# Graph attention in 128 rounds: the probability blocks of four graphs turned by one instruction a round, with their stores and the first and last rounds rearranged

## The reference, cut to what matters

```python
q, k, v = (split_heads(x @ W.T) for W in (Wq, Wk, Wv))
a = einsum('bhnd,bhmd->bhnm', q, k) * 512 ** -0.5 + 2 * adj     # spatial and edge encoding are both adj
a = where(any(a != 0, axis=-1), a, -inf)                        # rows that are all zero give p = 0
p = softmax(a)
o = einsum('bhnm,bhmd->bhnd', p, v)
out = layernorm(x + o @ Wo.T)                                   # no scale, no shift
```

## Time and profile before

| what | value |
|---|---|
| median of 3 runs | 1715.5 us (1714.86 to 1715.84) |
| the profiled execution's own time | 1715.16 us |
| its span | 1713.3 us |
| PE, DVE, ACT, POOL busy | 1697.4, 1633.3, 1369.0, 963.7 us |
| TensorE's granted clock | 0.998 of full |

### The profile page before, as it was taken

How to read it: one execution, slowest core, us unless ns; L and a number is a source line. 1 busy time by engine, 2 the same in 40 slices (tenths; PEclk the granted TensorE clock), 3 DMA queues, 4 the chain that set the end, 5 groups by cost and what they waited for, 6 DMA issues and landing times. The chain is left out here.

```text
span 1713.3 us, 45982 instructions
## 1 busy us (share of the span) xinstructions
PE 1697.4 (99%) x14385; PEld 1383.9 (81%) x14385; DVE 1633.3 (95%) x5814; ACT 1369.0 (80%) x5136; POOL 963.7 (56%) x1512
## 2 busy tenths in 40 slices
PE   9999999999999999999999999999999999999997
PEld 7788888888888888888888888888888888888875
DVE  7999999999999999999999999999999999999997
ACT  7777888788778877888788878877887788778876
POOL 2356556555565565555655655556556556565554
PEclk9999999999999999999999999999999999999999
DMA  7677777777777777777777777777777777777775
GB/s 239 194 216 217 227 232 226 225 221 231 226 223 226 225 224 227 226 218 238 215 229 227 224 229 219 225 233 221 230 222 226 227 225 231 225 215 230 226 228 163
DMA packets 275764, 382.61 MB, mean 223 GB/s; under 512 B 25152, under 2 KB 156480, under 8 KB 275392
## 3 DMA queue, kind: packets, MB, share of 16 engines
q1 hardware_dynamic: 275376, 379.42, 75.4%
q10 hardware_dynamic: 144, 0.26, 0.1%
HBM read 212.86 MB, written 166.72 MB: 222 GB/s over the span
## 5 line engine op out<-in xcount | busy, mean ns | idle before, releaser
L860 ACT ACTIVATE e_sb<-neg_a,neg_max 128x128 f32<-128x128 f32 x2048 | 793.1, 391 | 181.9 <-DVE neg_max L1043 181.9
L1043 DVE CUSTOM_DVE_ANT_0 neg_a<-ps_s,adj_sb 128x128 f32<-128x128 f32 x2048 | 440.2, 285 | 7.4 <-PE ps_s L657 5.9
L574 PE MATMUL ps_w<-xt_hi,w_lo 128*128 128x512 f32 x1020 | 412.5, 404 | 0.0
L575 PE MATMUL ps_w<-xt_lo,w_hi 128*128 128x512 f32 x1020 | 399.4, 392 | 0.0
L860 ACT ACTIVATION_READ_ACCUMULATOR e_sb<-neg_a,neg_max 128x1 f32 x2048 | 387.8, 189 | 0.0
L1099 DVE STREAM_TRANSPOSE e_b<-e_sb 128x1024 f32<-128x1024 f32 x254 | 316.3, 1245 | 27.3 <-DVE e_sb L1089 0.9
L1089 DVE SCALAR_TENSOR_TENSOR e_sb<-e_sb,r_inv 128x1024 f32<-128x1024 f32 x256 | 318.3, 1243 | 7.9 <-DVE r_inv L1083 0.2
L1051 DVE TENSOR_REDUCE neg_min<-neg_a 128x16 f32<-128x2048 f32 x128 | 292.7, 2287 | 4.4
L437 POOL TENSOR_TENSOR o_lo<-o_sb,o_hi 128x512 fp32r<-128x512 f32 x126 | 163.3, 1296 | 218.9 <-ACT o_sb L777 209.5
L577 PE MATMUL ps_w<-xt_hi,w_hi 128*128 128x512 f32 x1020 | 273.3, 390 | 0.0
L574 PEld LDWEIGHTS ps_w<-xt_hi,w_lo 128*128 128x128 f32 x1020 | 191.2, 187 | 57.6 <-issue 12.5
(11 more groups left out here) (125 smaller groups left out, 2796.9 us busy)
## 6 DMA issues: line engine op xcount, KB each, us to landing
blocks<-e_b SPq DMA_DIRECT2D x1016, 128.0 KB, 2.2
e_t<-blocks SPq DMA_DIRECT2D x126, 1024.0 KB, 7.4
x_sb<-x SPq DMA_DIRECT2D x121, 256.0 KB, 4.8
out<-x_sb SPq DMA_DIRECT2D x121, 256.0 KB, 3.4
xt_raw<-xt SPq DMA_DIRECT2D x120, 256.0 KB, 4.9
adj_sb<-adj SPq DMA_DIRECT2D x32, 256.0 KB, 5.4
neg_a<-xt SPq DMA_DIRECT2D x4, 256.0 KB, 4.8
v_sb<-wv SPq DMA_DIRECT2D x4, 256.0 KB, 7.2
```

Of the source, the lines that this page charges most:

```text
L574: pe.matmul(out, lhs_lo(c), rhs_hi(c), start=(c == 0), stop=False)
L575: pe.matmul(out, lhs_hi(c), rhs_lo(c), start=False, stop=False)
L860: last = act.activation(e_sb[:, i, h, :], neg_a[:, i, h, :], ACT.Exp, scale=-1.0, bias=neg_max[:, i, h:h + 1], accum_out=sums[:, i, h:h + 1])
L1043: last = dve.tensor_tensor_reduce(out=neg_a[:, i, h, :], in0=ps_s[h][:, i * NODES:(i + 1) * NODES], in1=adj_sb[:, g % PAIR, i, :], scale=- ...
```

## The change

`turn_blocks` is called once a round, after `normalise(f, 1)`, on all four graphs: one transpose of 2048 elements in place of two of 1024. The two `saved` semaphores become one, and e_b, the DRAM buffer and e_t lose the half index, so a band's row of blocks is 2 KB where it was two of 1 KB. `save_blocks(f)` issues four DMAs of 256 KB in place of eight of 128 KB; it stands where the second half's stood. `move_last` keeps its two DMAs, both behind all stores. `exps(f, 0)` now waits for the whole transpose.

At the start: the rest of v's last weight chunk goes from VectorE to GpSimd's first place; in round 3 ScalarE takes `values_hi(1)` behind all exponentials; in round 2 GpSimd holds `chunk_lo` back until `bias(3)` has begun. At the end: GpSimd does `ln(126)` in round 127, behind the additions and `values_lo(125)`, and ScalarE takes `values_hi(125)` ahead of `preload(3)`.

```diff
-        blocks = e_b[:, :].rearrange("p (m b r j) -> p m r b j", m=2, b=BLOCKS, r=2 * TH)
+        blocks = e_b[:, :].rearrange("p (b r j) -> p r b j", b=BLOCKS, r=GG * TH)
+        block_rows = e_b[:, :].rearrange("p (b c) -> p b c", b=BLOCKS)
...
             def move_last(half):
-                sp.wait_ge(saved[half], 16 * BLOCKS * (f + 1))
+                sp.wait_ge(saved, 16 * BLOCKS * (f + 1))
...
-            def save_blocks(f, half):
-                sp.wait_ge(transposed, 2 * f + half + 1)
+            def save_blocks(f):
+                sp.wait_ge(transposed, f + 1)
                 if f > 1:
                     sp.wait_ge(moved[f % PAIR], 16 * (f // PAIR))
                 for a in (0, 2, 1, 3):
                     rows = slice(BLOCK * a, BLOCK * (a + 1))
-                    sp.dma_start(blocks_d[f % 2, a, :, half].rearrange("(b j) c -> j b c", b=BLOCKS),
-                                 blocks_half[rows, half]).then_inc(saved[half], 16)
+                    sp.dma_start(blocks_d[f % 2, a].rearrange("(b j) c -> j b c", b=BLOCKS),
+                                 block_rows[rows]).then_inc(saved, 16)
...
             for f in range(PHASES):
                 if f:
-                    save_blocks(f - 1, 1)
+                    save_blocks(f - 1)
...
-                save_blocks(f, 0)
...
+            pool.wait_ge(wv_hi_done, CH)
+            rest(w_lo[:, WEIGHT["v"], CH - 1, :], w_stage["v"][:, CH - 1], w_hi[:, WEIGHT["v"], CH - 1, :]
+                 ).then_inc(wv_last_lo_done, 1)
...
                 if f == LAST - 1:
                     add(f, 1)
-                ln(f)
+                else:
+                    if f == LAST:
+                        ln(f - 1)
+                    ln(f)
+                if f == 2:
+                    pool.wait_ge(biased, GG * (f + 1) + 1)
                 chunk_lo(late_chunk(f))
...
             def exps(f, i):
-                if f and i % 2 == 0:
-                    act.wait_ge(transposed, 2 * (f - 1) + i // 2 + 1)
+                if f and i == 0:
+                    act.wait_ge(transposed, f)
...
-                    if i < len(valued(f)):
+                    if i < len(valued(f)) and valued(f)[i] != 1:
                         values_hi(valued(f)[i])
...
+                if f == TILES - 1:
+                    values_hi(1)
...
+            values_hi(LAST - 2)
             preload(3)
-            values_hi(LAST - 2)
...
-            def turn_blocks(f, half):
+            def turn_blocks(f):
                 if f:
-                    dve.wait_ge(saved[half], 16 * BLOCKS * f)
-                dve.wait_ge(normalised, 2 * f + half + 1)
-                dve.transpose(blocks[:, half],
-                              e_sb[:, 2 * half:2 * half + 2].rearrange("p i h (b j) -> p (i h) b j", b=BLOCKS)
+                    dve.wait_ge(saved, 16 * BLOCKS * f)
+                dve.wait_ge(normalised, 2 * f + 2)
+                dve.transpose(blocks, e_sb[:, :].rearrange("p i h (b j) -> p (i h) b j", b=BLOCKS)
                               ).then_inc(transposed, 1)
...
-            for c in range(CH):
+            for c in range(CH - 1):
                 dve.wait_ge(wv_hi_done, c + 1)
...
                 normalise(f, 0)
-                if f < LAST:
-                    turn_blocks(f, 0)
-                else:
+                if f == LAST:
                     stats(f - O_LAG - 1)
                     means(f - O_LAG - 1)
                 reciprocals(f, 1)
                 row_factors(f, 1)
                 normalise(f, 1)
                 if f < LAST:
-                    turn_blocks(f, 1)
+                    turn_blocks(f)
```

More of the change, by code:

```diff
@@ L179, in build @@
         last_tmp = sb("last_tmp", [P, 4, 2])
-        blocks = e_b[:, :].rearrange("p (m b r j) -> p m r b j", m=2, b=BLOCKS, r=2 * TH)
-        blocks_half = e_b[:, :].rearrange("p (m b c) -> p m b c", m=2, b=BLOCKS)
-        t_blocks = [e_t[:, n].rearrange("p (a m i h j) -> p a m i h j", a=BLOCKS, m=2, i=2, h=TH) for n in range(PAIR)]
+        blocks = e_b[:, :].rearrange("p (b r j) -> p r b j", b=BLOCKS, r=GG * TH)
+        block_rows = e_b[:, :].rearrange("p (b c) -> p b c", b=BLOCKS)
+        t_blocks = [e_t[:, n].rearrange("p (a i h j) -> p a i h j", a=BLOCKS, i=GG, h=TH) for n in range(PAIR)]
         t_plain = e_b[:, :].rearrange("p (i h n) -> p i h n", i=GG, h=TH)
@@ L201, in build @@
         wv_lo_done = sem("wv_lo_done")
+        wv_last_lo_done = sem("wv_last_lo_done")
         wo_hi_done = sem("wo_hi_done")
@@ L224, in build @@
         transposed = sem("transposed")
-        saved = [sem(f"saved{half}") for half in range(2)]
+        saved = sem("saved")
         moved = [sem(f"moved{n}") for n in range(PAIR)]
@@ L342, in move_last @@
                 f = LAST - 1
-                sp.wait_ge(saved[half], 16 * BLOCKS * (f + 1))
+                part = slice(2 * TH * BLOCK * half, 2 * TH * BLOCK * (half + 1))
+                sp.wait_ge(saved, 16 * BLOCKS * (f + 1))
                 sp.wait_ge(values_done, f - 1)
-                sp.dma_start(e_t[:, f % PAIR].rearrange("p (a m c) -> p a m c", a=BLOCKS, m=2)[:, :, half],
-                             blocks_d[f % 2].rearrange("a p m c -> p a m c")[:, :, half]).then_inc(last_moved[half], 16)
-            def save_blocks(f, half):
-                sp.wait_ge(transposed, 2 * f + half + 1)
+                sp.dma_start(e_t[:, f % PAIR].rearrange("p (a c) -> p a c", a=BLOCKS)[:, :, part],
+                             blocks_d[f % 2].rearrange("a p c -> p a c")[:, :, part]).then_inc(last_moved[half], 16)
+            def save_blocks(f):
+                sp.wait_ge(transposed, f + 1)
                 if f > 1:
@@ L354, in save_blocks @@
                     rows = slice(BLOCK * a, BLOCK * (a + 1))
-                    sp.dma_start(blocks_d[f % 2, a, :, half].rearrange("(b j) c -> j b c", b=BLOCKS),
-                                 blocks_half[rows, half]).then_inc(saved[half], 16)
+                    sp.dma_start(blocks_d[f % 2, a].rearrange("(b j) c -> j b c", b=BLOCKS),
+                                 block_rows[rows]).then_inc(saved, 16)
             def move_blocks(f):
-                for half in range(2):
-                    sp.wait_ge(saved[half], 16 * BLOCKS * (f + 1))
+                sp.wait_ge(saved, 16 * BLOCKS * (f + 1))
                 if f > 1:
@@ L365, in move_blocks @@
                 sp.dma_start(e_t[:, f % PAIR].rearrange("p (a c) -> p a c", a=BLOCKS),
-                             blocks_d[f % 2].rearrange("a p m c -> p a (m c)")).then_inc(moved[f % PAIR], 16)
+                             blocks_d[f % 2].rearrange("a p c -> p a c")).then_inc(moved[f % PAIR], 16)
             for c in range(CH):
@@ L610, in before @@
                         pe.wait_ge(wv_hi_done, c + 1)
-                        pe.wait_ge(wv_lo_done, c + 1)
+                        if c < CH - 1:
+                            pe.wait_ge(wv_lo_done, c + 1)
+                        else:
+                            pe.wait_ge(wv_last_lo_done, 1)
                     weight_product(kind, 0, index, before if index == 0 else None)
@@ L679, in values @@
                         cols = slice((TH * t + h) * HD, (TH * t + h + 1) * HD)
-                        weights = t_plain[:, i, h, :] if f == LAST else t_blocks[f % PAIR][:, :, i // 2, i % 2, h, :]
+                        weights = t_plain[:, i, h, :] if f == LAST else t_blocks[f % PAIR][:, :, i, h, :]
                         last = pe.matmul(out[HD * h:HD * (h + 1), i * P:(i + 1) * P],
@@ L864, in turned_out @@
             def turned_out(i):
-                for half in range(2):
-                    act.wait_ge(saved[half], 16 * BLOCKS * LAST)
+                act.wait_ge(saved, 16 * BLOCKS * LAST)
                 act.wait_ge(turned, i + 1)
@@ L980, in turned_out @@
             def turned_out(i):
-                for half in range(2):
-                    dve.wait_ge(saved[half], 16 * BLOCKS * LAST)
+                dve.wait_ge(saved, 16 * BLOCKS * LAST)
                 dve.wait_ge(turned, i + 1)
@@ L1184 @@
     out = nc.dram_tensor("out", [GROUPS, NODES, GG, D], F32, kind="ExternalOutput").ap()
-    blocks = nc.dram_tensor("blocks", [2, BLOCKS, P, 2, 2 * TH * BLOCK], F32, kind="Internal").ap()
+    blocks = nc.dram_tensor("blocks", [2, BLOCKS, P, GG * TH * BLOCK], F32, kind="Internal").ap()
     build(nc, *aps, out, blocks)
```

## The result

| | before | after |
|---|---|---|
| median (5 runs each, one chip) | 1714.86 us (1714.61 to 1715.84) | 1766.41 us (1759.01 to 1767.06) |
| profiled execution, its span | 1715.16, 1713.3 us | 1759.01, 1757.2 us |
| granted clock | 0.998 | 0.998 |

The ratio is 1.0285 [1.0272, 1.0297]: slower, by 51.5 us in the medians. Forecast were 1731 us and a range up to 1747. The direction was right, the cost three times as high.

A forecast was written before the change was run, and what follows sets the result against it. TensorE's work was taken as the bound, 26.34 us per pair of rounds. VectorE's lag +10, late stores and moves +8, start +1 and end -3 made +16 us, forecasting 1731 us, range 1711.5 to 1747.

The forecast's parts named there:

- What bounds the kernel: Rounds in the middle: TensorE's work sets 26.34 us for an even and an odd round together, 61 times.
- The slack of the move: Probabilities' way to TensorE: the median move lands 1.0 us before use; the slowest landing, 10.3 us, would miss.
- VectorE's order: One late transpose of 2310 ns: even rounds 0.28 us shorter, odd 0.80 longer, +0.17 a pair past the cushion; +10 us.
- the bias of even rounds: VectorE, start of even rounds: `bias` would no longer be released by TensorE's scores.
- The stores: All 1 MB starts behind the transpose and lands 0.7 us later; four in ten moves late by 0.4 us; +8 us.
- rival (b): Store bands limited to 245 GB/s, landing 2.3 us later, nearly every move stalls: +73, 1760 us or more; chance 0.05.
- Two costs that add: TensorE's stalls for moves give VectorE part of its lag back, so the late-move cost of +10 counts as +8.
- GpSimd against VectorE: Even rounds: `row_factors` L1083 meets GpSimd's power L479; priced 0, otherwise up to 0.4 us a round, +24 us.
- rival (c): L1083 collides with L479 in even rounds: +24 less what stalls gave back, about 1747 us; chance 0.11.
- Ends: First and last rounds: +1 us at the start from TensorE's doubled wait, -3 at the end from reordered work.
- The wait for the last bank: TensorE near the end: with `ln(126)` behind the additions, all of its 2.06 us wait goes.

The follow-up runs named there:

- plain store: The changed kernel with the DRAM buffer laid out as e_b: one 1 MB store from all 128 partitions, the move in four DMAs of 256 KB; 1744.56 us.
- the two late: The kernel before, with its first transpose moved behind the second `normalise`, still two transposes and eight stores; 1732.60 us.
- blocks alone: The changed kernel with the first and last rounds' order of the kernel before; 1766.92 us, ratio 1.0300.

## Why the prediction was right or wrong

**What bounds the kernel: right.** TensorE's work sets the 26.34, and the loss came as its waits. The slack of the move was put at 1.0 us: by the means it was 13.0 - 11.84 = 1.2.

**VectorE's order: right in its steps, and near in its price.** The transpose takes 2311 ns (forecast 2310). Even rounds are 0.29 us shorter (0.28), odd ones 0.73 longer (0.80). The reciprocal waits for ScalarE, 1.02 us at the place shown. A pair is 0.21 longer with this order alone (0.17). Its 10 us are 16.3 with the transfers alike, and 17.7 in the kernel before, in which the first half's later stores are contained (0.9 us behind T). That the bias of even rounds would no longer be released by TensorE was wrong where TensorE stalls: it then is the late one.

**The stores: this step failed, by its size.** The prediction took 0.7 us for the later landing, "nearer the lower end, since half the bytes in flight no longer come as 1 KB rows", and with it +8 in the sum. They land 2.4 us later in the mean, at its upper end of 2.3, and late stores alone cost 34.1 us. Two windows had been read as if the length of rows made the rate, 245 against 408 GB/s. But the first was of stores from bands and the second was of a move and other loads; with rows of 1 KB the changed kernel's blocks are as late and the time is the same, while another layout brings 2.2 us back. So it was the bands and the bytes, and the row with the higher rate didn't apply to any store of the change. That is rival (b), which I gave a chance of 0.05, with 1760 or more. Its number was met partly by luck: it priced the stores at +73 less something regained, up to twice what they cost alone, and the rest came from VectorE's order. The move itself takes 7.03 us in place of 7.50, so of the 2.4 us 1.9 arrive at TensorE. That is more than the slack of 1.2, and 39 of the 58 odd rounds stall, by 0.9, where the forecast had 24 or so of 0.4.

**Two costs that add.** The prediction let the stalls give VectorE's lag back, and took 8 for 10. Here the two give nothing back: 34.1 for the stores and 16 to 18 for the order make the whole. That fits the table, where both reach TensorE by the landing of the move and by nothing else; a run that separates them further wasn't made.

**A stall costs more than its wait:** some 0.2 us more, 39 times, at a full clock. It was in no term. What TensorE does in these 0.2 us isn't shown.

**GpSimd against VectorE: right in the middle, missed at the end.** L1083 (now L1095) beside L479 was priced 0, and even rounds have the length forecast without a collision. The trace shows it directly. GpSimd and VectorE in round 60:

```profile
831.09 0.55 POOL L479 TENSOR_TENSOR ln_tmp<-ln_tmp,constants 128x1 f32<-128x1 f32 x1
```

```profile
831.29 0.17 DVE L1095 SCALAR_TENSOR_TENSOR r_inv<-recip,nonzero 128x8 f32<-128x8 f32 x1
```

It starts inside L479 in 58 rounds, and takes its 0.17 us in each. So rival (c) is out. What was missed stands at the end, where an addition was held by `normalise`.

**Ends: right alone, wrong together.** Forecast +1 - 3; alone they bring -3.2. In the changed kernel the stretch ahead of round 7 is 1.4 us longer, near the +1, but the one behind round 123 is 1.0 longer where 3 shorter was forecast. The wait for the last bank, of which "all of the 2.06 goes", is 2.10 against 2.06 before. Two things there were in no term: the addition held for 1.04 us, and the clock, at 0.50 for 3.4 us behind that wait, which by my estimate loses half of it, 1.7 us.

**Open:** whether the ends still gain anything beside the late blocks; and whether a move in one piece with a plain store would be early enough, which was not tried, since the layout of one makes bands of the other.

## What to carry to other kernels

A piece of work inside a wait of its engine is free, and merging it with its later twin takes it out of there: VectorE's transposes fell from 316.3 to 293.5 us of busy time, and the kernel became 16 us slower by it, the transfers being alike. When a half that used to leave early now leaves with the late one, ask what the transfer of everything takes from that moment until it has landed, and hold it against the slack of whoever needs it. A rate read from a window belongs to the transfers in it, with their partitions: take it for others only if they touch as many.

## What the runs showed of the hardware

- 1 MB from SBUF to DRAM took 5.34 us in four bands of 32 partitions and 4.05 in four transfers from all 128, alone on the chip. Rows of 1 or 2 KB made no difference (5.41, 5.34).
- The issue of four stores of 256 KB from bands took 2.54 us on SP's queue, of four of 128 KB 1.77. Alone on the chip the four took 0.30, 0.43, 0.68 and 0.98 us, four of the same size from all 128 partitions 0.32, 0.43, 0.46 and 0.45: it isn't the size alone. Why the issue gets longer isn't shown.
- Beside a GpSimd subtraction of 128x512 `row_factors` took 1.05 us (57 rounds of the changed kernel), beside GpSimd's power of 128x1 its usual 0.17 (58 rounds).
- Stores whose outermost dimension is 4 kept 0.26 of the DMA engines busy (88 GB/s), and the kernel took 2221 us.
- Two transposes behind each other are no slower in their chain than one of twice the size, though the engine is busy a little longer. In the kernel with the two late, its VectorE:

```profile
818.99 1.22 DVE L1089 SCALAR_TENSOR_TENSOR e_sb<-e_sb,r_inv 128x1024 f32<-128x1024 f32 x1
820.13 2.36 DVE L1099 STREAM_TRANSPOSE e_b<-e_sb 128x1024 f32<-128x1024 f32 x2
```

  From the end of `normalise` to that of the transposes are 822.49 - 820.21 = 2.28 us; in the changed kernel 849.38 - 846.96 = 2.42. The first of two depends on the first half only and starts 0.08 before `normalise` has ended; the merged one waits for it and starts 0.11 behind. Whole rounds agree: 12.25 and 14.22 against 12.38 and 14.36.
- The clock: in the window at 1729.20, just behind the stall of 2.10 us for the last bank, TensorE was granted 0.50, its lower level of 1.2 GHz, where it had 1.00 before; behind the stall of 2.06 in the kernel before it kept 1.00. In the slowest execution of "blocks alone" (1771.06 us) three such stretches lie between rounds 7 and 123. A pair without one, the next pair with one, and the stretch itself, behind a stall of 2.14 us:

```profile
1136.30:1163.30 27.00, 27.00 (x231) 21.70 (x229) 25.28 (x90) 21.24 (x80) 17.00 (x26) 1.00 0.71 209
1163.30:1193.50 30.20, 28.06 (x229) 22.65 (x228) 25.45 (x89) 21.46 (x80) 13.45 (x25) 0.94 0.71 217
1167.51:1170.92 3.41, 3.34 (x36) 2.69 (x37) 3.38 (x13) 3.27 (x13) 1.27 (x1) 0.50 0.92 285
```

  The five executions of the changed kernel had mean clocks of 0.994 to 0.999, the kernel before, over all of its executions here, 0.997 to 0.999. By my estimate 0.001 of the mean is 1.8 us of TensorE's 1766, so 0.998 against 0.994 is 7 us, about the spread between 1759 and 1767 us; the single executions don't line up by it exactly (1761.68 at 0.999 lies above 1759.01 at 0.998), so it isn't the clock alone.
